# A graph layer with layer norm on one core: first adjacency block in two halves, scale factors of the last tiles in two chains

## The chip, the core and the metric

The kernel runs on one core of a Trainium2 chip. A core has TensorE (PE in the profile), VectorE (DVE), ScalarE (ACT), GpSimd (POOL) and SyncE (SP), each with its own stream of instructions; they wait for one another by semaphores. Sixteen DMA engines move data between HBM and the on-chip SBUF. TensorE writes to PSUM. The metric is the device time of one execution, in microseconds (us).

## What is computed

```python
support = x @ weight                      # x 4096x256, weight 256x256
y = (1 - t) * support + t * (adj @ support)   # adj 4096x4096, t one number
out = layernorm(x + y, axis=-1)           # eps 1e-5
```

## The kernel before

The product is reordered as z = t (adj x) + (1 - t) x, then z W. Each float32 operand is split into a high part of type fp32r (ScalarE or VectorE casts it) and a low part, the difference (VectorE, for early x GpSimd). A product is three matmuls: high by high, high by low, low by high. Output nodes are worked in 8 chunks of 512; per chunk the 32 blocks of 128 input nodes come in 8 groups of 4. One group is an adjacency tile of 1 MB in a ring of four slots (a_raw, a_hi, a_lo) and 24 matmuls of 512 columns into agg[chunk parity][feature half]. Chunks 0 and 1 alternate by group, so that x is used as it arrives.

At the start the first tiles come in small pieces. FIRST_RUN (L18) packs them in HBM in the order in which SyncE loads them (L204 to L221): x block 0, adjacency blocks 0 of slots 0 and 1, x block 1, and so on. Each has its own semaphore. Ten warm-up matmuls of 512 columns on constants (L675) stand ahead of the first useful one. The first adjacency block is loaded in one DMA; ScalarE casts its left 256 columns (L278), VectorE its right 256 (L469), VectorE subtracts all 512 (L464), and fine_piece (L565) issues six matmuls of 512 columns, with waits for hi, x_lo (GpSimd, L335) and lo between the pairs. The fifth piece (index 4) is the first that piece (L584) handles.

At the end project_last (L628) multiplies the last z by W in four tiles of 128 nodes; tiles 2 and 3 get the centred features added on TensorE by an identity matrix (L652, L653). VectorE adds the features of tiles 0 and 1 (L529), ScalarE sums their squares (L318), VectorE takes the statistics of tiles 2 and 3 (L533, L536). Then one chain works on a 128x4 array of all four tiles: VectorE adds eps (L539), takes the reciprocal (L541), multiplies by ScalarE's root (L544, L322) and does one Newton step (L546, L549). ScalarE scales tiles 2 and 3 (L325) and issues their stores (L329); VectorE scales 0 and 1 (L554) and SyncE issues theirs (L243).

The order on each engine is the order of the code; nothing reorders it.

Of the kernel before, what the change touches and what calls it, by code (L numbers as in the profile page):

```python
# [6 lines left out]
P = 128  # L7
WIDE = 512
GROUP = 4
# [3 lines left out]
WARM = 10  # L13
FINE = 4
# [9 lines left out]
def gnn_layernorm_kernel(nc, x_rows, first_run, xT, adjT, t, W, out):  # L24
# [33 lines left out]
    with ctx:  # L58
# [53 lines left out]
        first_hi_ready = sem("first_hi_ready")  # L112
# [26 lines left out]
        inv_var_ready = sem("inv_var_ready")  # L139
        act_stored = sem("act_stored")  # L140
# [19 lines left out]
        def adj_source(q):  # L160
            n = A_PIECES[q][2]
            first = run_offset("a", q)
            return first_run[first:first + n * P * WIDE].rearrange("(p b w) -> p b w", p=P, b=n)

        def load_and_store(sp):
# [12 lines left out]
            def load_adj(n):  # L178
                slot, turn = n % RING, n // RING
                c, g = chunk_group(n)  # L180
                if turn == 1:
                    sp.wait_ge(a0_lo_ready, a_after(slot))
# [22 lines left out]
            load_adj_piece(0)  # L205
# [40 lines left out]
            sp.wait_ge(stored[1], 16 * (CHUNKS // 2 - 1 + 2))  # L246
            sp.wait_ge(act_stored, 16 * 2)

        def scalar_engine(act):
# [22 lines left out]
            def root(c):  # L272
# [82 lines left out]
        def vector_engine(dve):  # L355
# [105 lines left out]

            def a_low_piece(q):
# [265 lines left out]
```

## Time and profile before

| what | us |
|---|---|
| median of 3 runs (lowest, highest) | 383.89 (383.85, 384.13) |
| the profiled execution's own time | 383.85 |
| its span in the trace | 382.6 |
| TensorE matmuls busy, 1686 instructions | 376.6 (98%) |
| VectorE busy | 237.6 (62%) |
| ScalarE busy | 145.7 (38%) |
| GpSimd busy | 22.2 (6%) |

Busy is the time in which an engine has an instruction running. Matmuls overlap: one of 512 columns is listed with 389 ns while the next begins after about 0.23 us, so the step between starts is what it costs. The transfers run at 258 to 420 GB/s over the first 57 us and at about half of that later. The granted TensorE clock is shown as full in all 40 slices; the pace of the first six microseconds is read from the steps between weight loads. PEld is the weight load, which overlaps the matmul before it; SPq and ACTq are the queues on which an engine issues DMAs.

### The profile page before, as it was taken

How to read it: one execution, taken by the hardware profiler on the slowest of the kernel's cores; microseconds unless marked ns; L12 is line 12 of the kernel's file. 1: busy time of each engine (PE TensorE's matmuls, PEld its weight loads, DVE VectorE, ACT ScalarE, POOL GpSimd, SP SyncE). 2: the span in 40 equal slices, each digit the busy share in tenths (PEclk: the TensorE clock that was granted, in tenths of full speed). 3: DMA queues.
4: the chain of work that ended last, by engine and by line, in shares of the span. 5: the costliest groups of instructions: out<-in, count | busy, mean ns of one | idle time of the engine just before them, and what ended most of it. 6: DMA issues, size and time to landing. Idle time of an engine off the chain costs nothing.

```text
span 382.6 us, 4167 instructions
## 1 busy us (share of the span) xinstructions
PE 376.6 (98%) x1686; PEld 310.8 (81%) x1686; DVE 237.6 (62%) x335; ACT 145.7 (38%) x114; POOL 22.2 (6%) x19
## 2 busy tenths in 40 slices
PE   9999999999999999999999999999999999999994
PEld 5888888888888888888888888888888888888884
DVE  4978955447879466844577446873477643697305
ACT  4767544243352434324424325244332344423102
POOL 1202300003000010000100001000100001000000
PEclk9999999999999999999999999999999999999999
DMA  7999997555465766557665666756647567321001
GB/s 258 418 392 418 415 420 265 190 217 207 179 231 208 257 217 233 184 214 258 218 202 194 208 244 212 243 197 213 212 179 274 174 267 270 119 106 55 2 0 56
DMA packets 19107, 84.42 MB, mean 221 GB/s; under 512 B 1936, under 2 KB 6800, under 8 KB 11408
## 3 DMA queue, kind: packets, MB, share of 16 engines
q1 hardware_dynamic: 18656, 83.89, 59.7%
q10 hardware_dynamic: 432, 0.26, 0.2%
q8 instruction: 13, 0.21, 0.2%
q14 instruction: 6, 0.05, 0.0%
HBM read 79.95 MB, written 4.19 MB: 220 GB/s over the span
## 4 chain that ended last, share of the span: by engine, by line
PE 98%; DVE 1%; ACT 0%; issue 0%; DVEq 0%
PE agg L563 30%; PE agg L562 30%; PE agg L561 30%; PE out_ps L624 3%; PE out_ps L625 2%; PE out_ps L676 1%; PE agg L573 1%; PE agg L577 1%; PE agg L581 0%; ACT x_raw L325 0%; DVE x_raw L529 0%; DVE stats L533 0%; PE out_ps L645 0%; PE out_ps L647 0%; PE out_ps L646 0%
## 5 line engine op out<-in xcount | busy, mean ns | idle before, releaser
L359 DVE TENSOR_TENSOR a_lo<-a_raw,a_hi 128x2048 fp32r<-128x2048 f32 x60 | 137.4, 2291 | 111.1 <-ACT a_hi L263 111.1
L561 PE MATMUL agg<-a_hi,x_hi 128*128 128x512 f32 x504 | 196.3, 389 | 0.0
L563 PE MATMUL agg<-a_hi,x_lo 128*128 128x512 f32 x504 | 196.2, 389 | 0.0
L562 PE MATMUL agg<-a_lo,x_hi 128*128 128x512 f32 x504 | 196.1, 389 | 0.0
L263 ACT ACTIVATE a_hi<-a_raw 128x2048 fp32r<-128x2048 f32 x60 | 114.7, 1913 | 129.0 <-PE agg L563 123.7
L561 PEld LDWEIGHTS agg<-a_hi,x_hi 128*128 128x128 f32 x504 | 94.6, 188 | 19.8
L563 PEld LDWEIGHTS agg<-a_hi,x_lo 128*128 128x128 f32 x504 | 94.6, 188 | 19.8
L562 PEld LDWEIGHTS agg<-a_lo,x_hi 128*128 128x128 f32 x504 | 94.6, 188 | 19.6
L340 POOL TENSOR_TENSOR xt<-xt,omt_col 128x1024 f32<-128x1024 f32 x8 | 18.1, 2257 | 292.4 <-DMA xt<-in_xT 292.4
L624 PE MATMUL out_ps<-w_split,z_hi 128*128 128x512 f32 x56 | 20.0, 397 | 0.0
L274 ACT ACTIVATE std<-var_eps 128x4 f32<-128x4 f32 x7 | 1.4, 206 | 47.7 <-DVE var_eps L400 47.7
L270 ACT ACTIVATE z_hi<-z 128x512 fp32r<-128x512 f32 x14 | 8.8, 633 | 26.8 <-DVE z L372 21.7
L625 PE MATMUL out_ps<-w_split,z_lo 128*128 128x256 f32 x56 | 15.7, 280 | 0.0
L464 DVE TENSOR_TENSOR a_lo<-a_raw,a_hi 128x512 fp32r<-128x512 f32 (+1 forms) x12 | 11.3, 961 | 2.6 <-ACT a_hi L257 2.2
L624 PEld LDWEIGHTS out_ps<-w_split,z_hi 128*128 128x128 f32 x56 | 10.5, 188 | 2.5
L372 DVE SCALAR_TENSOR_TENSOR z<-agg,t_col,xt 128x512 f32<-128x512 f32 x14 | 10.4, 747 | 2.8 <-PE agg L563 2.8
L378 DVE TENSOR_TENSOR z_lo<-z,z_hi 128x512 fp32r<-128x512 f32 x14 | 9.5, 688 | 2.7 <-ACT z_hi L270 2.1
L625 PEld LDWEIGHTS out_ps<-w_split,z_lo 128*128 128x128 f32 x56 | 10.6, 189 | 0.3
L428 DVE TENSOR_TENSOR x_lo<-x_raw,x_hi 128x1024 fp32r<-128x1024 f32 (+1 forms) x8 | 10.5, 1310 | 0.1
L257 ACT ACTIVATE a_hi<-a_raw 128x512 fp32r<-128x512 f32 (+1 forms) x11 | 8.7, 789 | 4.7 <-DMA a_raw<-in_first_run 4.6
L387 DVE TENSOR_TENSOR x_raw<-out_ps,rows 128x256 f32<-128x256 f32 x28 | 9.9, 416 | 0.0
L391 DVE TENSOR_TENSOR x_raw<-out_ps,x_raw 128x256 f32<-128x256 f32 x28 | 9.9, 415 | 0.0
(76 smaller groups left out, 95.9 us busy)
## 6 DMA issues: line engine op xcount, KB each, us to landing
a_raw<-in_adjT SPq DMA_DIRECT2D x60, 1024.0 KB, 4.8
xt<-in_xT SPq DMA_DIRECT2D x8, 512.0 KB, 5.6
rows<-in_x SPq DMA_DIRECT2D x8, 512.0 KB, 5.7
out<-x_raw SPq DMA_DIRECT2D x7, 512.0 KB, 2.9
x_raw<-in_first_run SPq DMA_DIRECT2D x6, 512.0 KB, 11.9
a_raw<-in_first_run SPq DMA_DIRECT2D x8, 256.0 KB, 4.6
a_raw<-in_first_run SPq DMA_DIRECT2D x4, 512.0 KB, 7.3
x_raw<-in_first_run SPq DMA_DIRECT2D x4, 128.0 KB, 3.9
```

The costliest lines, as they stand in the source:

```text
L263: nc.scalar.activation(a_hi[:, slot], a_raw[:, slot], ACT.Copy).then_inc(a_hi_ready[slot], 1)
L340: nc.gpsimd.tensor_tensor(xt[:, c % 2], xt[:, c % 2], omt_col[:, :].unsqueeze(2).broadcast_to([P, KT, WIDE]), ALU.mult).then_inc(xt_scaled, 1)
L359: nc.vector.tensor_tensor(a_lo[:, slot], a_raw[:, slot], a_hi[:, slot].bitcast(f32), ALU.subtract).then_inc(a_lo_ready[slot], 1)
L372: nc.vector.scalar_tensor_tensor(z[:, k], agg[c % 2][k][:, :], t_col[:, :], xt[:, c % 2, k], ALU.mult, ALU.add).then_inc(z_ready[k], 1)
L387: nc.vector.tensor_tensor(y_tile(i), out_ps[i][:, 0:feats], rows[:, c % 2, i], ALU.add).then_inc(part_ready, 1)
L428: nc.vector.tensor_tensor(x_lo[:, j:j + n], x_part(x_raw, p), x_hi[:, j:j + n].bitcast(f32), ALU.subtract).then_inc(x_lo_ready, 1)
L464: nc.vector.tensor_tensor(a_part(a_lo, q), a_part(a_raw, q), a_part(a_hi, q).bitcast(f32), ALU.subtract).then_inc(a0_lo_ready, 1)
L561: nc.tensor.matmul(bank, x_hi[:, j, cols], a_hi[:, slot, b], start=first, stop=False)
L562: nc.tensor.matmul(bank, x_hi[:, j, cols], a_lo[:, slot, b], start=False, stop=False)
L563: return nc.tensor.matmul(bank, x_lo[:, j, cols], a_hi[:, slot, b], start=False, stop=last)
L624: nc.tensor.matmul(out_ps[i][:, :], z_hi[:, k, cols], w_split[:, k], start=(k == 0), stop=False)
L625: done = nc.tensor.matmul(dst, z_lo[:, k, cols], w_hi[:, k], start=False, stop=(k == KT - 1))
```

## The change

The warm-ups become seven. The first adjacency block is stored in HBM as two blocks of 256 columns and loaded in two DMAs, each with a semaphore. VectorE casts half 0, ScalarE half 1, VectorE subtracts each, and TensorE does six matmuls of 256 columns on half 0 and then six on half 1. The counts of the waits on a0_hi_ready and a0_lo_ready move by one accordingly.

At the end the 128x4 chain becomes two 128x2 chains, for tiles 0 and 1 (early) and tiles 2 and 3 (late), with their rows alternating on VectorE, and two roots on ScalarE. ScalarE scales tiles 0 and 3, VectorE 2 and 1; SyncE stores 0, 2, 1 and ScalarE stores 3. One identity matmul of tile 3 moves behind the products of tile 2.

```diff
-WARM = 10
+WARM = 7
+HALF = WIDE // 2
...
             load_x(0)
-            load_adj_piece(0)
+            for h in range(2):
+                sp.dma_start(first_block(a_raw, h), first_block_source(h)).then_inc(half_loaded[h], 16)
             load_adj_piece(1)
...
-            for i in range(2):
-                sp.wait_ge(normed_ready, c * TILES + i + 1)
-                sp.dma_start(out[c * WIDE + i * P:c * WIDE + (i + 1) * P], normed(c)[:, i]
-                             ).then_inc(stored[c % 2], 16)
+            sp.wait_ge(act_normed_ready, 1)
+            sp.dma_start(out[c * WIDE:c * WIDE + P], normed(c)[:, 0]).then_inc(stored[c % 2], 16)
+            sp.wait_ge(normed_ready, c * TILES + 1)
+            sp.dma_start(out[c * WIDE + 2 * P:c * WIDE + 3 * P], normed(c)[:, 2]).then_inc(stored[c % 2], 16)
+            sp.wait_ge(normed_ready, c * TILES + 2)
+            sp.dma_start(out[c * WIDE + P:c * WIDE + 2 * P], normed(c)[:, 1]).then_inc(stored[c % 2], 16)
...
-            act.wait_ge(a0_loaded[0], 16)
-            nc.scalar.activation(a_hi[:, 0, 0, 0:WIDE // 2], a_raw[:, 0, 0, 0:WIDE // 2], ACT.Copy
-                                 ).then_inc(a0_hi_ready, 1)
+            act.wait_ge(half_loaded[1], 16)
+            nc.scalar.activation(first_block(a_hi, 1), first_block(a_raw, 1), ACT.Copy).then_inc(half_hi_ready[1], 1)
...
+            nc.scalar.activation(std[:, early], mean_var[:, early, 1], ACT.Sqrt, bias=eps_col[:, :]
+                                 ).then_inc(early_std_ready, 1)
             act.wait_ge(mean_var_ready, c * TILES + 2)
-            nc.scalar.activation(std[:, :], mean_var[:, :, 1], ACT.Sqrt, bias=eps_col[:, :]).then_inc(std_ready, 1)
+            nc.scalar.activation(std[:, late], mean_var[:, late, 1], ACT.Sqrt, bias=eps_col[:, :]).then_inc(std_ready, 1)
+            act.wait_ge(early_rstd_ready, 1)
+            nc.scalar.activation(normed(c)[:, 0], y_tile(0), ACT.Copy, scale=rstd[:, 0:1]).then_inc(act_normed_ready, 1)
             act.wait_ge(rstd_ready, c + 1)
-            for i in (2, 3):
-                nc.scalar.activation(normed(c)[:, i], out_ps[i][:, 0:feats], ACT.Copy, scale=rstd[:, i:i + 1]
-                                     ).then_inc(act_normed_ready, 1)
-            for i in (2, 3):
-                act.wait_ge(act_normed_ready, i - 1)
-                act.dma_start(out[c * WIDE + i * P:c * WIDE + (i + 1) * P], normed(c)[:, i]).then_inc(act_stored, 16)
+            nc.scalar.activation(normed(c)[:, 3], out_ps[3][:, 0:feats], ACT.Copy, scale=rstd[:, 3:4]
+                                 ).then_inc(act_normed_ready, 1)
+            act.wait_ge(act_normed_ready, 2)
+            act.dma_start(out[c * WIDE + 3 * P:c * WIDE + 4 * P], normed(c)[:, 3]).then_inc(act_stored, 16)
...
+            def a_low_half(h):
+                dve.wait_ge(half_hi_ready[h], 1)
+                nc.vector.tensor_tensor(first_block(a_lo, h), first_block(a_raw, h), first_block(a_hi, h).bitcast(f32),
+                                        ALU.subtract).then_inc(a0_lo_ready, 1)
+
...
             x_high(0)
-            dve.wait_ge(a0_loaded[0], 16)
-            nc.vector.tensor_copy(a_hi[:, 0, 0, WIDE // 2:], a_raw[:, 0, 0, WIDE // 2:]).then_inc(first_hi_ready, 1)
-            dve.wait_ge(first_hi_ready, 1)
-            a_low_piece(0)
+            dve.wait_ge(half_loaded[0], 16)
+            nc.vector.tensor_copy(first_block(a_hi, 0), first_block(a_raw, 0)).then_inc(half_hi_ready[0], 1)
+            for h in range(2):
+                a_low_half(h)
...
-            for i in (2, 3):
-                dve.wait_ge(stats_ready, c * TILES + i - 1)
-                nc.vector.bn_aggr(mean_var[:, i], stats[:, i]).then_inc(mean_var_ready, 1)
             dve.wait_ge(square_ready, 2)
+            nc.vector.tensor_scalar(var_eps[:, early], mean_var[:, early, 1], EPS, None, ALU.add
+                                    ).then_inc(early_var_ready, 1)
+            dve.wait_ge(stats_ready, c * TILES + 1)
+            nc.vector.bn_aggr(mean_var[:, 2], stats[:, 2]).then_inc(mean_var_ready, 1)
+            dve.wait_ge(early_var_ready, 1)
+            nc.vector.reciprocal(inv_var[:, early], var_eps[:, early]).then_inc(early_inv_ready, 1)
+            dve.wait_ge(stats_ready, c * TILES + 2)
+            nc.vector.bn_aggr(mean_var[:, 3], stats[:, 3]).then_inc(mean_var_ready, 1)
+            dve.wait_ge(early_inv_ready, 1)
+            dve.wait_ge(early_std_ready, 1)
+            nc.vector.tensor_tensor(rstd0[:, early], inv_var[:, early], std[:, early], ALU.mult
+                                    ).then_inc(early_rstd0_ready, 1)
             dve.wait_ge(mean_var_ready, c * TILES + 2)
-            nc.vector.tensor_scalar(var_eps[:, :], mean_var[:, :, 1], EPS, None, ALU.add).then_inc(var_eps_ready, 1)
+            nc.vector.tensor_scalar(var_eps[:, late], mean_var[:, late, 1], EPS, None, ALU.add).then_inc(var_eps_ready, 1)
+            dve.wait_ge(early_rstd0_ready, 1)
+            nc.vector.scalar_tensor_tensor(newton_q[:, early], std[:, early], -0.5, rstd0[:, early], ALU.mult, ALU.mult
+                                           ).then_inc(early_q_ready, 1)
             dve.wait_ge(var_eps_ready, c + 1)
-            nc.vector.reciprocal(inv_var[:, :], var_eps[:, :]).then_inc(inv_var_ready, 1)
+            nc.vector.reciprocal(inv_var[:, late], var_eps[:, late]).then_inc(inv_var_ready, 1)
+            dve.wait_ge(early_q_ready, 1)
+            nc.vector.scalar_tensor_tensor(rstd[:, early], newton_q[:, early], 1.5, rstd0[:, early], ALU.add, ALU.mult
+                                           ).then_inc(early_rstd_ready, 1)
             dve.wait_ge(inv_var_ready, 1)
             dve.wait_ge(std_ready, c + 1)
...
-            nc.vector.tensor_tensor(rstd0[:, :], inv_var[:, :], std[:, :], ALU.mult).then_inc(rstd0_ready, 1)
+            nc.vector.tensor_tensor(rstd0[:, late], inv_var[:, late], std[:, late], ALU.mult).then_inc(rstd0_ready, 1)
...
             dve.wait_ge(rstd_ready, c + 1)
             dve.wait_ge(stored[c % 2], 16 * (c // 2))
-            for i in (0, 1):
-                nc.vector.tensor_scalar(normed(c)[:, i], y_tile(i), rstd[:, i:i + 1], None, ALU.mult
-                                        ).then_inc(normed_ready, 1)
+            nc.vector.tensor_scalar(normed(c)[:, 2], out_ps[2][:, 0:feats], rstd[:, 2:3], None, ALU.mult
+                                    ).then_inc(normed_ready, 1)
+            dve.wait_ge(early_rstd_ready, 1)
+            nc.vector.tensor_scalar(normed(c)[:, 1], y_tile(1), rstd[:, 1:2], None, ALU.mult).then_inc(normed_ready, 1)
...
+            def first_piece_half(h):
+                cols = slice(h * HALF, (h + 1) * HALF)
+                pe.wait_ge(x0_hi_ready, 1)
+                pe.wait_ge(half_hi_ready[h], 1)
+                for k in range(KT):
+                    nc.tensor.matmul(agg[0][k][:, cols], x_hi[:, 0, k * P:(k + 1) * P], first_block(a_hi, h),
+                                     start=(h == 0), stop=False)
+                pe.wait_ge(x0_lo_ready, 1)
+                for k in range(KT):
+                    nc.tensor.matmul(agg[0][k][:, cols], x_lo[:, 0, k * P:(k + 1) * P], first_block(a_hi, h),
+                                     start=False, stop=False)
+                pe.wait_ge(a0_lo_ready, h + 1)
+                for k in range(KT):
+                    nc.tensor.matmul(agg[0][k][:, cols], x_hi[:, 0, k * P:(k + 1) * P], first_block(a_lo, h),
+                                     start=False, stop=False)
+
...
                 pe.wait_ge(x0_hi_ready, b + 1)
-                pe.wait_ge(a0_hi_ready, q + 1)
-                if q == 0:
-                    pe.wait_ge(first_hi_ready, 1)
+                pe.wait_ge(a0_hi_ready, q)
...
+                def add_features(i, part):
                     cols = slice((i - 2) * feats, (i - 1) * feats)
-                    nc.tensor.matmul(dst, ident[:, :], centred_part(a_hi)[:, cols], start=False, stop=False)
-                    nc.tensor.matmul(dst, ident[:, :], centred_part(a_lo)[:, cols], start=False, stop=False)
+                    nc.tensor.matmul(out_ps[i][:, 0:feats], ident[:, :], part[:, cols], start=False, stop=False)
...
-                for i in (2, 3):
-                    add_features(i)
+                add_features(2, centred_part(a_hi))
+                add_features(2, centred_part(a_lo))
+                add_features(3, centred_part(a_hi))
...
-                for i in (2, 3):
-                    high_times_weights(i)
-                    low_times_weights(i)
+                high_times_weights(2)
+                low_times_weights(2)
+                add_features(3, centred_part(a_lo))
+                high_times_weights(3)
+                low_times_weights(3)
...
             bf16 = mybir.dt.bfloat16
             for _ in range(WARM):
...
-            for q in range(FINE):
+            for h in range(2):
+                first_piece_half(h)
+            for q in range(1, FINE):
                 fine_piece(q)
```

On SyncE's queue at the start (128 partitions by elements per partition):

```order
L173 DMA x_raw<-in_first_run 128x256
L176 DMA a_raw<-in_first_run 128x512 x2
L173 DMA x_raw<-in_first_run 128x256
L176 DMA a_raw<-in_first_run 128x512 x2
L173 DMA x_raw<-in_first_run 128x256
```

and now

```order
L185 DMA x_raw<-in_first_run 128x256
L218 DMA a_raw<-in_first_run 128x256 x2
L188 DMA a_raw<-in_first_run 128x512
L185 DMA x_raw<-in_first_run 128x256
L188 DMA a_raw<-in_first_run 128x512 x2
L185 DMA x_raw<-in_first_run 128x256
```

Every load behind the first block stands one issue further back. On TensorE at the start, where agg00 and agg01 are the two feature halves of chunk 0, before

```order
L676 MATMUL out_ps0<-const-bfloat16-1.0 128x512 x10
L573 MATMUL agg00<-a_hi,x_hi 128x512
L573 MATMUL agg01<-a_hi,x_hi 128x512
L577 MATMUL agg00<-a_hi,x_lo 128x512
L577 MATMUL agg01<-a_hi,x_lo 128x512
L581 MATMUL agg00<-a_lo,x_hi 128x512
L581 MATMUL agg01<-a_lo,x_hi 128x512
```

and now

```order
L728 MATMUL out_ps0<-const-bfloat16-1.0 128x512 x7
L607 MATMUL agg00<-a_hi,x_hi 128x256
L607 MATMUL agg01<-a_hi,x_hi 128x256
L611 MATMUL agg00<-a_hi,x_lo 128x256
L611 MATMUL agg01<-a_hi,x_lo 128x256
L615 MATMUL agg00<-a_lo,x_hi 128x256
L615 MATMUL agg01<-a_lo,x_hi 128x256
L607 MATMUL agg00<-a_hi,x_hi 128x256
```

Six matmuls became twelve of half the width, the second six for half 1. On VectorE at the end, from the statistics of tile 3 on (out_ps3), before

```order
L533 BN_STATS stats<-out_ps3 128x6
L536 BN_AGGR mean_var<-stats 128x2 x2
L539 TENSOR_SCALAR var_eps<-mean_var 128x4
L541 RECIPROCAL inv_var<-var_eps 128x4
L544 TENSOR_TENSOR rstd0<-inv_var,std 128x4
L546 SCALAR_TENSOR_TENSOR newton_q<-std,rstd0 128x4
L549 SCALAR_TENSOR_TENSOR rstd<-newton_q,rstd0 128x4
L554 TENSOR_SCALAR x_raw<-x_raw,rstd 128x256 x2
```

and now

```order
L556 TENSOR_SCALAR var_eps<-mean_var 128x2
L559 BN_AGGR mean_var<-stats 128x2
L561 RECIPROCAL inv_var<-var_eps 128x2
L563 BN_AGGR mean_var<-stats 128x2
L566 TENSOR_TENSOR rstd0<-inv_var,std 128x2
L569 TENSOR_SCALAR var_eps<-mean_var 128x2
L571 SCALAR_TENSOR_TENSOR newton_q<-std,rstd0 128x2
L574 RECIPROCAL inv_var<-var_eps 128x2
L576 SCALAR_TENSOR_TENSOR rstd<-newton_q,rstd0 128x2
L580 TENSOR_TENSOR rstd0<-inv_var,std 128x2
L582 SCALAR_TENSOR_TENSOR newton_q<-std,rstd0 128x2
L585 SCALAR_TENSOR_TENSOR rstd<-newton_q,rstd0 128x2
```

Ten short rows stand where five stood, and two of the early chain's are ahead of the aggregation of tile 3 (L563).

## Rows read from the trace of the kernel before

**Rows 1.** The page: chain that ended last, by engine; costliest groups, one of TensorE's.
```profile
PE 98%; DVE 1%; ACT 0%; issue 0%; DVEq 0%
...
L561 PE MATMUL agg<-a_hi,x_hi 128*128 128x512 f32 x504 | 196.3, 389 | 0.0
```
**Rows 2.** Timeline (start us, length us, engine, line), 0 to 12 us, TensorE.
```profile
0.84 4.42 PE L676 MATMUL out_ps<-const-bfloat16-1.0 128*128 128x512 bf16 x10 [0.84 <-PEq L722]
...
4.63 0.33 PEld L573 LDWEIGHTS agg<-a_hi,x_hi 128*128 128x128 f32 x1 [0.28 <-issue]
5.06 0.33 PEld L573 LDWEIGHTS agg<-a_hi,x_hi 128*128 128x128 f32 x1
...
6.34 0.21 PEld L581 LDWEIGHTS agg<-a_lo,x_hi 128*128 128x128 f32 x1
6.61 0.19 PEld L581 LDWEIGHTS agg<-a_lo,x_hi 128*128 128x128 f32 x1
...
10.92 0.19 PEld L561 LDWEIGHTS agg<-a_hi,x_hi 128*128 128x128 f32 x1
11.14 0.39 PE L561 MATMUL agg<-a_hi,x_hi 128*128 128x512 f32 x1
```
**Rows 3.** Timeline, 0 to 5 us, the other engines.
```profile
1.25 0.42 SPq L176 DMA_DIRECT2D a_raw<-in_first_run  x1
1.71 0.42 SPq L176 DMA_DIRECT2D a_raw<-in_first_run  x1
...
2.95 0.29 DVE L423 CAST x_hi<-x_raw 128x256 fp32r<-128x256 f32 x1 [2.95 <-DMA x_raw<-in_first_run]
3.33 0.73 POOL L335 TENSOR_TENSOR x_lo<-x_raw,x_hi 128x256 fp32r<-128x256 f32 x1 [2.82 <-DVE x_hi L423]
3.79 0.42 ACT L278 ACTIVATE a_hi<-a_raw 128x256 fp32r<-128x256 f32 x1 [1.70 <-DMA a_raw<-in_first_run]
3.80 0.40 DVE L469 CAST a_hi<-a_raw 128x256 fp32r<-128x256 f32 x1 [0.55 <-DMA a_raw<-in_first_run]
```
**Rows 4.** Timeline, 7.7 to 10.7 us, pieces three and five.
```profile
7.76 0.69 DVE L464 TENSOR_TENSOR a_lo<-a_raw,a_hi 128x512 fp32r<-128x512 f32 x1 [1.26 <-ACT a_hi L257]
...
8.73 0.63 ACT L257 ACTIVATE a_hi<-a_raw 128x512 fp32r<-128x512 f32 x1 [0.36 <-DMA a_raw<-in_first_run]
...
9.38 0.74 POOL L335 TENSOR_TENSOR x_lo<-x_raw,x_hi 128x256 fp32r<-128x256 f32 x1 [2.06 <-DVE x_hi L423]
...
9.40 1.27 DVE L464 TENSOR_TENSOR a_lo<-a_raw,a_hi 128x512 fp32r<-128x512 f32 x1
```
**Rows 5.** Stretches; last columns: granted TensorE clock, DMA share, GB/s.
```profile
8.00:9.00 1.00, 1.00 (x6) 0.84 (x5) 1.00 (x2) 0.64 (x2) 0.00 (x0) 1.00 1.00 353
```
**Rows 6.** Timeline, 377 to 381 us, all engines.
```profile
377.20 0.28 PE L638 MATMUL out_ps<-w_split,z_lo 128*128 128x256 f32 x1
...
377.51 0.43 DVE L533 BATCH_NORM_STATS2 stats<-out_ps 128x6 f32<-128x256 f32 x1
...
377.86 0.30 DVE L536 BATCH_NORM_AGGREGATE mean_var<-stats 128x2 f32<-128x6 f32 x2
...
378.27 0.17 DVE L539 TENSOR_SCALAR var_eps<-mean_var 128x4 f32<-128x4 f32 x1
...
379.28 0.84 ACT L325 ACTIVATE x_raw<-out_ps,rstd 128x256 f32<-128x256 f32 x2 [0.72 <-DVE rstd L549]
...
379.66 0.34 SPq L243 DMA_DIRECT2D out<-x_raw  x1
...
380.05 0.43 SPq L243 DMA_DIRECT2D out<-x_raw  x1
...
380.17 0.45 ACTq L329 DMA_DIRECT2D out<-x_raw  x1
```
**Rows 7.** Chain of waits in order of time (start us, us), one product of tile 0.
```profile
376.05 0.12 PE out_ps L633
```
**Rows 8.** DMA view of 379 to 383 us, in 40 slices of 0.1 us.
```profile
GB/s 0 0 82 0 0 0 0 0 0 0 0 0 0 0 0 256 358 338 338 307 358 338 348 318 369 358 318 348 348 338 185 21 0 0 0 0 0 0 0 0
```

More of the change, by code:

```diff
@@ L110, in gnn_layernorm_kernel @@
         out_ps = [ctx.enter_context(nc.psum_tensor(f"out_ps{i}", [P, WIDE], f32)) for i in range(TILES)]
-        first_hi_ready = sem("first_hi_ready")
+        half_loaded, half_hi_ready = sems("half_loaded", 2), sems("half_hi_ready", 2)
         w_loaded, w_hi_ready, w_lo_ready = sem("w_loaded"), sem("w_hi_ready"), sem("w_lo_ready")
@@ L139, in gnn_layernorm_kernel @@
         inv_var_ready = sem("inv_var_ready")
+        early_var_ready, early_inv_ready, early_std_ready = sem("early_var_ready"), sem("early_inv_ready"), sem("early_std_ready")
+        early_rstd0_ready, early_q_ready, early_rstd_ready = sem("early_rstd0_ready"), sem("early_q_ready"), sem("early_rstd_ready")
         act_stored = sem("act_stored")
@@ L149, in x_part, with first_block @@
             return buf[:, j // GROUP % X_RING, j % GROUP:j % GROUP + n]
+        def first_block(buf, h):
+            return buf[:, 0, 0, h * HALF:(h + 1) * HALF]
         def run_offset(kind, index):
@@ L163, in adj_source, with first_block_source @@
             return first_run[first:first + n * P * WIDE].rearrange("(p b w) -> p b w", p=P, b=n)
+        def first_block_source(h):
+            first = run_offset("a", 0) + h * P * HALF
+            return first_run[first:first + P * HALF].rearrange("(p w) -> p w", p=P)
+        early, late = slice(0, 2), slice(2, TILES)
         def load_and_store(sp):
@@ L181, in load_adj @@
                 if turn == 1:
-                    sp.wait_ge(a0_lo_ready, a_after(slot))
+                    sp.wait_ge(a0_lo_ready, a_after(slot) + 1)
                 else:
@@ L543, in vector_engine @@
             dve.wait_ge(std_ready, c + 1)
-            nc.vector.tensor_tensor(rstd0[:, :], inv_var[:, :], std[:, :], ALU.mult).then_inc(rstd0_ready, 1)
+            nc.vector.tensor_tensor(rstd0[:, late], inv_var[:, late], std[:, late], ALU.mult).then_inc(rstd0_ready, 1)
             dve.wait_ge(rstd0_ready, c + 1)
-            nc.vector.scalar_tensor_tensor(newton_q[:, :], std[:, :], -0.5, rstd0[:, :], ALU.mult, ALU.mult
+            nc.vector.scalar_tensor_tensor(newton_q[:, late], std[:, late], -0.5, rstd0[:, late], ALU.mult, ALU.mult
@@ L547, in vector_engine @@
                                            ).then_inc(newton_q_ready, 1)
             dve.wait_ge(newton_q_ready, c + 1)
-            nc.vector.scalar_tensor_tensor(rstd[:, :], newton_q[:, :], 1.5, rstd0[:, :], ALU.add, ALU.mult
+            nc.vector.scalar_tensor_tensor(rstd[:, late], newton_q[:, late], 1.5, rstd0[:, late], ALU.add, ALU.mult
                                            ).then_inc(rstd_ready, 1)
@@ L578, in fine_piece @@
                                      start=False, stop=False)
-                pe.wait_ge(a0_lo_ready, q + 1)
+                pe.wait_ge(a0_lo_ready, q + 2)
                 for k in range(KT):
@@ L586, in piece @@
                 c, g = chunk_group(slot)
-                pe.wait_ge(a0_lo_ready, q + 1)
+                pe.wait_ge(a0_lo_ready, q + 2)
                 if g == 0:
@@ L716 @@
             slot, b, n = A_PIECES[index]
-            first_run.append(adjT[slot % 2 * (blocks // GROUP) + slot // 2, :, b:b + n].ravel())
+            halves = [slice(0, HALF), slice(HALF, WIDE)] if index == 0 else [slice(0, WIDE)]
+            for cols in halves:
+                first_run.append(adjT[slot % 2 * (blocks // GROUP) + slot // 2, :, b:b + n, cols].ravel())
     first_run = np.concatenate(first_run)
```

8 lines of the change are left out of this document (3 added, 5 removed).

## The prediction, made before the changed kernel ran

> **What bounds the kernel now.** I read the page's chain of waits first. TensorE holds 98% of it, and in the costliest groups its matmuls show no idle time before them [rows 1]. So a microsecond counts only where TensorE works slowly or has nothing to do: ahead of the steady stream, and after its last matmul. The timeline of the first 12 us shows the first. Ten warm-up matmuls on constants start at 0.84 us; weight loads then follow at the pace of one 512-column matmul, 0.43 us (4.63 to 5.06), and still do to 6.34; from 6.34 to 6.61 the step is 0.27 us, and afterwards it is 0.23 (10.92 to 11.14 is one step) [rows 2]. 512 columns in 0.43 us is the 1.2 GHz level, in 0.22 us the 2.4 GHz level; the rise lies near 6.4 us, after 5.5 us of unbroken matmuls. Useful work begins in the array at 5.06 us.
>
> The timeline of the end shows the other: the last matmul ends at 377.20 + 0.28 = 377.48 us, and the span at 382.6. Those 5.1 us are the normalisation of the last four tiles on VectorE and ScalarE, and the stores [rows 6]. So at most about 6 us are open to this change; the rest is 5.44 us per 24 matmuls, which it leaves alone.
>
> **Warm-ups and halves.** Three warm-ups fewer free 3 x 0.43 = 1.28 us of slow time: the seven end at 5.06 - 1.28 = 3.78 us. At half pace that is worth 0.64 us at most, and only if data are there at once. They are not. In the kernel before, x is seen at 2.95 and the 256 KB block at 3.80 [rows 3]. Half 0 is 128 KB behind x; half of that 0.85 us gives 3.38 us. Its cast runs on VectorE. The same cast of x took 0.29 us, the one of the block 0.40, beside GpSimd's x_lo, which runs from 3.33 to 4.06 [rows 3]. The same pair shows again at 9.4: a subtraction of 512 columns takes 0.69 us alone and 1.27 us when x_lo started 0.02 us before it, ending 0.55 us after x_lo's end [rows 4]. That is not slowing in proportion; VectorE stood still until GpSimd was done. So the half's cast, started at 3.38 against x_lo at 3.33, should end about 0.15 us after 4.06, at 4.2, where it ended before. If it wins by arriving earlier, it ends at 3.7. I take 4.2. The Trainium skill (SBUF — State Buffer, "Who interferes with whom") states this as a lock: whichever of the two starts first holds the shared port pair for its whole instruction, and the other fully blocks. The trace agrees, in both places; by a proportional sharing of the port the cast would end at about 3.9 and TensorE would begin 0.3 us earlier.
>
> TensorE then gets half 0 at 4.24, streams from about 4.45 (a weight load of 0.33 us lies ahead of the first matmul), and has idled some 0.6 us. Against 5.06 this is 0.6 us earlier at half pace: 0.3 us in full-speed terms. Twelve matmuls of 256 columns carry the columns of six of 512. At the fast level one of 256 steps by 0.12 us [rows 7] against 0.23 for 512, so each split costs 0.01: at most 6 x 0.01 = 0.06, and I take 0.03. The other inputs are in time: x_lo at 4.06, half 1 by ScalarE at 3.79 + 0.42 = 4.21 or one more landing later, a_lo of half 0 some 0.45 us after 4.2, needed at 4.9. Head start at the second block: 0.27 us (0.1 to 0.6).
>
> **What the head start meets.** Pieces keep arriving at the pace of the transfers. The tightest one is the fifth adjacency piece. ScalarE idles 0.36 us for its landing and splits it at 8.73; VectorE's a_lo of it starts at 9.40, behind x_lo as told above, and is ready at 10.67; TensorE's weight load for it goes at 10.92 and its matmul streams at 11.14 [rows 2, 4]. Weight loads run one matmul ahead; with an idle array about 0.1 us of it is enough. So TensorE could have started that piece at 10.67 + 0.05 + 0.1 = 10.82 in place of 11.14: 0.3 us is the most that a head start can bring through here, if the piece comes no later. It comes later: the halves are one more DMA and rows of 1 KB instead of 2 KB. From below this costs 0: four stores of 128 KB in 1 KB rows moved in 1.7 us, 0.42 each [rows 8], and two of them equal the block's 0.85. From above it costs the spacing of two issues on SyncE's queue, 0.46 us (1.25 to 1.71) [rows 3]. The transfer engines are full in these microseconds (share 1.00 in 8 to 9 us) [rows 5], so the issue hides in their backlog and I take 0.15 for row overhead and one more completion. The piece is then ready at 10.97 and its matmul streams near 11.0 to 11.05: the gain that passes is 0.1 us (-0.15 to +0.3). Behind this place the pieces are needed every 1.36 us and come faster; nothing else is near. The steady stream then runs unchanged, 0.1 us earlier.
>
> **The tail.** TensorE's last work: one matmul on the identity moves from ahead of tile 0's products to ahead of tile 3's. Tiles 0 to 2 end 0.12 us earlier [rows 7], tile 3 not at all. VectorE's statistics of tile 3 start at 377.51, 0.03 us after TensorE's end at 377.48 [rows 6], so they stay. From there VectorE had two aggregations from 377.86, five dependent steps of 0.20 us each from 378.27, and the scaling at 379.28. Now the first aggregation has a row of tiles 0 and 1 ahead of it, and a reciprocal that itself waits 0.2 us stands ahead of the second, which so starts near 378.13 in place of 377.98. The five late steps follow with the early chain's rows in the 0.2 us gaps: late factors 0.1 us later (0 if all hides, 0.3 if each of five inserted rows adds 0.06), so scaling at 379.38. Early factors are ready near 378.88, 0.4 us before the old ones.
>
> Stores before: issues at 379.66 and 380.05 on SyncE, the last at 380.17 on ScalarE [rows 6]. Data move from 380.5 to 382.2 without a pause [rows 8]: 0.85 us after the first issue, 0.42 us per tile. The rate of the transfers, not the last issue, sets the end. Now: ScalarE scales tile 0 from 378.88, SyncE issues it at 379.33; tile 2 follows at 379.38 + 0.38 = 379.76 (the lag of scaling to issue in rows 6), tile 3 from ScalarE at 379.38 + 0.52 = 379.90 (one scaling of about 0.47, two take 0.84, and 0.05 to the issue), tile 1 at 379.76 + 0.46 = 380.22. Data: tile 0 from 380.18 to 380.60, where tile 2 is just ready, then three times 0.42: 381.87. Tile 1 could have begun at 381.07 and doesn't decide. Gain 382.2 - 381.87, less a little for holes between issues: 0.27 us (0 to 0.4).
>
> **Sum.** 383.85 (this execution, span 382.6 and 1.25 around it) - 0.1 - 0.27 = 383.48; the median of the runs, 383.89, gives 383.52. Forecast 383.5, own range 383.2 to 383.8.
>
> **Rivals.** (a) Both ends pay in full: the fifth piece arrives no later or its subtraction misses x_lo (0.58 us less), the head start is 0.45, the tail 0.35: 383.85 - 0.8 = 383.05. For it: the block's time equals two halves of a store. Against it: the order of VectorE's rows around that piece is the same. (b) The tail gives nothing: three stores in one queue, the last issued at 380.22 or, with the longer chain, 380.4, against 380.17. If the end tracks the last issue, it is 0.05 to 0.2 us later: 383.85 - 0.1 + 0.1 = 383.85. For it: the last store landed 2.0 us after its issue. Against it: the unbroken transfer of rows 8. (c) Slower: the clock. TensorE now idles some 0.6 us between warm-ups and half 0. Before, the rise came after 5.5 us of unbroken matmuls. If the hole makes it come 5.5 us after 4.1, at 9.6 in place of 6.4, TensorE works 5.15 us at half pace (4.45 to 9.6), 2.6 us of full-speed work; before it had done 0.67 + 3.2 = 3.9 by then. It is 1.3 us behind, less the tail's 0.27: 384.85. It decides from a rise about 0.8 us late on. For it: no warm-up matmul covers the hole. Against it: the hole is a tenth of those microseconds. The Trainium skill (TensorE: Matmul & The Clock Gate, "What you observe") has the rise around 4 us into sustained matmuls, give or take 0.5 us from run to run; this trace shows 5.5 us. A rise 0.5 us late would cost 0.25 us at the second block, most of which the wait for the fifth piece absorbs.
>
> **How the numbers follow.** This kernel's runs tell a change from none at about 0.2%, 0.77 us: faster is below 383.12, slower above 384.66. Forecast 54%, (a) 17%, (b) 20%, (c) 9%. Forecast and (b) are no change; (a) is spread around the bound, and I give 16% to faster in all; (c) all slower: 0.16, 0.75, 0.09. The range takes in (a), (b) and small delays of the clock: 382.9 to 384.05.
>
> **What would show it.** Right: the half's cast ends near 4.2 us; TensorE idles after the seventh warm-up; its step halves near 6.4; a wait appears ahead of the fifth piece near 10.9; from 12 us on TensorE is 0.1 us earlier; the second aggregation starts 0.6 us after tile 3's statistics; data of the stores end 4.4 us after TensorE's last matmul, against 4.7. Wrong: a cast at 3.7 us with no hole; no wait at the fifth piece and a gain of 0.4 us or more by 12 us; steps of 0.43 us beyond 7 us; a pause in the transfers of the stores.

## The result and the profile after

The changed kernel is slower: 384.04 us median (383.48 to 384.79, 22 runs) against 383.62 us (382.88 to 384.13, 22 runs of before), ratio 1.0015, 95% interval 1.0009 to 1.0021. (The 383.89 shown earlier was the median of three of these.) The forecast was 383.5, that is 0.37 us less than the 383.89 it started from, with 0.75 on no change and 0.09 on slower; 384.04 lies at the upper edge of its range (384.05). Measured side by side the change costs 0.42 us by the medians and 0.6 us by the ratio, which is clear of noise and still less than the 0.2% from which the prediction counts a change as slower. A few executions of these series took far longer at a granted clock well below full, one of two_dma_2k for instance 639.53 us and the profiled one of tail_act_35 878.59; the ratios leave them out. The changed kernel's profiled execution took 384.10 us, span 382.9, against 383.85 and 382.6.

The chain of waits (shares by engine, then by line) no longer belongs to TensorE alone:

```profile
PE 96%; DMA 1%; DVE 1%; SPq 1%; issue 0%; ACT 0%
```

Before it read PE 98% [rows 1]. The new links are in the first 12 us. The chain of the stretches 2 to 7 and 9 to 12.5 us, in order of time (start us, us, what):

```profile
1.71 0.42 SPq L218
...
4.07 0.43 SPq L185
...
4.55 4.85 DMA a_raw<-in_first_run
...
9.42 0.64 ACT a_hi L272
...
10.09 1.24 DVE a_lo L485
...
11.37 0.50 PE agg L598
```

It starts at the issue of half 1, runs through SyncE's issues to the load of the fifth piece, and from there through its two splits to TensorE. The timeline (start us, us, engine, line; in brackets idle time before and what ended it) has the rows that answer to [rows 2 to 4]:

```profile
3.29 0.72 POOL L351 TENSOR_TENSOR x_lo<-x_raw,x_hi 128x256 fp32r<-128x256 f32 x1 [2.79 <-DVE x_hi L439]
3.44 0.73 DVE L490 CAST a_hi<-a_raw 128x256 fp32r<-128x256 f32 x1 [0.22 <-DMA a_raw<-in_first_run]
...
4.31 0.55 PE L607 MATMUL agg<-a_hi,x_hi 128*128 128x256 f32 x1 [0.33 <-DVE a_hi L490]
...
6.37 0.33 PEld L615 LDWEIGHTS agg<-a_lo,x_hi 128*128 128x128 f32 x1
6.59 0.26 PEld L615 LDWEIGHTS agg<-a_lo,x_hi 128*128 128x128 f32 x1
6.78 0.19 PEld L624 LDWEIGHTS agg<-a_hi,x_hi 128*128 128x128 f32 x1
...
9.42 0.63 ACT L272 ACTIVATE a_hi<-a_raw 128x512 fp32r<-128x512 f32 x1 [0.40 <-DMA a_raw<-in_first_run]
...
10.09 1.23 DVE L485 TENSOR_TENSOR a_lo<-a_raw,a_hi 128x512 fp32r<-128x512 f32 x1
...
11.37 0.50 PE L598 MATMUL agg<-a_hi,x_hi 128*128 128x512 f32 x1 [0.23 <-DVE a_lo L485]
```

The cast of half 0 took 0.73 us beside GpSimd and ended at 4.17. The first useful matmul is listed from 4.31, and the second weight load, which marks the first matmul in the array, goes at 4.45; before it went at 5.06 [rows 2]. So useful work began 0.6 us earlier, at the 1.2 GHz level. The step of a 256-column matmul is 0.21 to 0.22 us until 6.59, 0.19 there and shorter after. The first matmul of the second block shows what is left of the head start. Changed kernel, then the kernel before:

```profile
6.89 0.40 PE L624 MATMUL agg<-a_hi,x_hi 128*128 128x512 f32 x1
...
7.07 0.39 PE L573 MATMUL agg<-a_hi,x_hi 128*128 128x512 f32 x1
```

That is 0.18 us. (The weight loads for these two, at 6.78 and 6.84, can't be compared: each goes one matmul ahead, and the matmul between has 256 columns in one kernel and 512 in the other.) The fifth piece was split from 9.42, before from 8.73: 0.69 us later. TensorE waited and reached it at 11.37 in place of 11.14. Its weight load came with that matmul in place of ahead of it, and the end of the last matmul is 377.90, before 377.48: 0.42 us later.

The end of the kernel, rows that answer to [rows 6]:

```profile
377.62 0.28 PE L689 MATMUL out_ps<-w_split,z_lo 128*128 128x256 f32 x1
...
377.93 0.43 DVE L554 BATCH_NORM_STATS2 stats<-out_ps 128x6 f32<-128x256 f32 x1
...
378.55 0.16 DVE L563 BATCH_NORM_AGGREGATE mean_var<-stats 128x2 f32<-128x6 f32 x1
...
379.73 0.48 DVE L589 TENSOR_SCALAR x_raw<-out_ps,rstd 128x256 f32<-128x256 f32 x1
...
379.79 0.34 SPq L255 DMA_DIRECT2D out<-x_raw  x1
...
380.24 0.36 SPq L257 DMA_DIRECT2D out<-x_raw  x1
...
380.65 0.45 SPq L259 DMA_DIRECT2D out<-x_raw  x1
```

and the DMA view of 379 to 383 us in slices of 0.1 us [rows 8]:

```profile
GB/s 0 0 0 0 0 0 0 0 0 0 0 0 0 0 0 0 174 317 358 317 123 215 358 348 328 348 338 338 328 328 348 358 267 51 0 0 0 0 0 0
```

Data move from 380.6 to 382.4, with a dent at 381.0 where tile 0 has gone and tile 2 has not yet come. They end 4.5 us after TensorE's last matmul, before 4.7. Start and end together: +0.42 - 0.15 = +0.27 of the span.

### The profile page after: what moved, and what is told of

Same layout as the page of the kernel before. It is cut to its first block, busy times and chain, and to the rows that moved or that the text cites. A ratio compares the mean times of both kernels' runs of the same rounds, so it can differ in the third digit from the quotient of the medians.

```text
span 382.9 us, 4180 instructions
## 1 busy us (share of the span) xinstructions
PE 376.5 (98%) x1689; PEld 311.1 (81%) x1689; DVE 239.0 (62%) x341; ACT 146.2 (38%) x115; POOL 22.5 (6%) x19
## 4 chain that ended last, share of the span: by engine, by line
PE 96%; DMA 1%; DVE 1%; SPq 1%; issue 0%; ACT 0%
PE agg L598 30%; PE agg L600 30%; PE agg L599 30%; PE out_ps L675 3%; PE out_ps L676 2%; DMA a_raw<-in_first_run 1%; SPq L188 0%; SPq L185 0%; DVE a_lo L485 0%; SPq L218 0%; ACT a_hi L272 0%; PE out_ps L684 0%; PE out_ps L689 0%; DVE x_raw L589 0%; PE out_ps L696 0%
## 5 line engine op out<-in xcount | busy, mean ns | idle before, releaser
L433 DVE TENSOR_SCALAR x_raw<-x_raw,mean_var,rstd 128x256 f32<-128x256 f32 x28 | 9.7, 409 | 0.3
```

## Experiments

"Issued" is the time at which SyncE issues the load of the fifth piece, "fifth" the start of ScalarE's split of it, "rise" the time at which the step of TensorE halves, "GB/s" what the transfers moved from 2 to 7 us, "last" the end of the last matmul, each in the one profile of the kernel. Ratios are to the kernel before on the same chip. One profile is one execution: that of one_dma_1k, for instance, is the slowest of its eleven runs (384.16 us, median 383.66).

| kernel | ratio (95%) | rise | issued | fifth | GB/s | last |
|---|---|---|---|---|---|---|
| before | 1 | 6.4 | 4.07 | 8.73 | 303 | 377.48 |
| the change | 1.0015 (1.0009-1.0021) | 6.7 | 4.55 | 9.42 | 273 | 377.90 |
| tail_only | 0.9992 (0.9984-1.0001) | 5.4 | 4.06 | 8.41 | 310 | 377.03 |
| tail_again | 1.0002 (0.9993-1.0011) | 5.8 | 4.07 | 8.16 | 313 | 377.26 |
| start_only | 1.0016 (1.0007-1.0025) | 4.8 | 4.55 | 9.22 | 237 | 377.65 |
| start_warm10 | 1.0015 (1.0007-1.0024) | 6.7 | 4.54 | 10.54 | 251 | 378.47 |
| warm7_only | 1.0003 (0.9990-1.0016) | 8.7 | 4.06 | 8.96 | 308 | 378.40 |
| warm4_only | 1.0043 (1.0028-1.0058) | 8.5 | 4.07 | 8.70 | 307 | 378.31 |
| one_dma_1k | 1.0002 (0.9994-1.0011) | 6.0 | 4.10 | 9.45 | 303 | 377.82 |
| one_load | 1.0003 (0.9994-1.0012) | 3.7 | 4.07 | 8.56 | 318 | 377.00 |
| two_dma_2k | 1.0024 (1.0015-1.0033) | 6.7 | 4.98 | 9.59 | 210 | 378.03 |
| extra_small | 1.0015 (1.0006-1.0024) | 5.9 | 4.35 | 9.56 | 260 | 377.97 |
| start_xlo | 1.0019 (1.0010-1.0027) | 4.1 | 4.54 | 9.01 | 260 | 377.48 |
| two_dma_act | 1.0015 (1.0006-1.0023) | 4.0 | 4.58 | 9.99 | 204 | 378.47 |
| half1_act | 1.0038 (1.0026-1.0051) | 9.0 | 4.05 | 8.87 | 271 | 378.54 |
| after_act | 1.0020 (1.0006-1.0034) | 8.8 | 3.59 | 9.10 | 310 | 378.93 |
| after_act10 | 0.9999 (0.9990-1.0008) | 5.3 | 3.59 | 8.37 | 325 | 377.15 |
| tail_act | 0.9997 (0.9988-1.0006) | 3.7 | 3.64 | 8.61 | 305 | 376.99 |
| after_merge | 1.0029 (1.0017-1.0040) | 4.6 | 4.11 | 9.42 | 224 | 378.33 |
| tail_act_35 | 1.0026 (1.0014-1.0039) | - | - | - | - | - |

**Which half costs.** tail_only and tail_again are the kernel before with only the lines of the diff on the last four tiles (roots, chains, scalings, stores, identity matmul); start_only has all its other lines and the old end.

> Only the last four tiles are changed (two chains, stores, identity matmul); the start is that of before. Theory S (the start costs, the tail gives): 0.2 us less than before, ratio near 0.9995; the data of the last stores end about 4.5 us after TensorE's last matmul against 4.7. Theory T (the tail costs, for instance by its third store in one queue): 0.3 to 0.5 us more. In its profile the first piece of TensorE's wait at the fifth adjacency piece is absent, as before.

> The changed end with the start of before, once more. If the end gives 0.2 to 0.3 us: ratio 0.9992 to 0.9995 again, and below 1 with the first measurement together. If the first was chance: 1.0000.

> Only the start is changed (two half loads, seven warm-ups, twelve matmuls of 256 columns); the end is that of before. Theory S: 0.6 us more than before (0.42 for the whole change and the 0.2 that the tail gives back), with the fifth piece's landing 0.5 to 0.7 us later than 8.7 us and TensorE waiting for it. Theory T: within 0.1 us of before. Theory R (the late landings in the profile are chance of one run): landings spread over the same times as before, time within 0.1 us.

The start costs all of it: ratio 1.0016, 384.00 us against 383.63, which is 0.4 us by the medians and 0.6 by the ratio. Its profile has the same late fifth piece (9.22), but there TensorE loses more at the third: its weight load for that one goes at 8.25 after 1.19 us of idling, and the wait at the fifth is 0.32 us. The end is between -0.3 us and nothing: the two ratios average 0.9997. From TensorE's last matmul to the end of the span pass 4.95 to 4.96 us in the seven profiles with the new end, 5.08 to 5.15 in ten with the old one (5.34 in two more); that is a gain of 0.15 us, less than the first run suggested.

**Warm-ups or loads.** start_warm10 and warm7_only:

```diff
-WARM = 7        # start_only -> start_warm10
+WARM = 10
-WARM = 10       # before -> warm7_only
+WARM = 7
```

> The changed start with ten warm-ups, the end of before. If the loads are what costs, TensorE again waits at the fifth piece and the time is that of start_only within 0.1 us (about 0.6 us above before). If the missing three warm-ups are what costs (clock), the time is near before.

> The kernel before with seven warm-ups in place of ten. If the clock's rise depends on unbroken work, it comes later than 6.4 us and the time is 0.3 us or more above before. If not, TensorE idles from 3.8 to 4.25 us, starts useful work 0.3 us earlier in full-speed terms than with ten, and the wait at the fifth piece takes all but about 0.3 us of it: 0.0 to 0.3 us less than before.

With ten warm-ups the changed start is as slow as with seven (384.16 and 384.00). With the old loads, seven cost nothing on average (383.63), but the runs spread from 382.79 to 385.76, and the profile, of an execution of 384.75 us, has the rise at 8.7 us. So the loads cost, and the warm-ups leave something else behind, taken up below.

**Rows, halves or one more DMA.** one_dma_1k keeps one DMA and makes its rows 1 KB; two_dma_2k keeps the rows and makes two DMAs; one_load has the halved work on one load; extra_small adds a DMA that carries next to nothing.

```diff
-            load_adj_piece(0)                                   # one_dma_1k
+            sp.dma_start(a_raw[:, 0, 0].rearrange("p (h w) -> p h w", h=2), ...rearrange("(h p w) -> p h w", h=2, p=P))
-            load_adj_piece(0)                                   # two_dma_2k
+            for h in range(2):
+                sp.dma_start(a_part(a_raw, 0)[part], adj_source(0)[part]).then_inc(a0_loaded[0], 16)
-            for h in range(2):                                  # start_only -> one_load
-                sp.dma_start(first_block(a_raw, h), first_block_source(h)).then_inc(half_loaded[h], 16)
+            load_adj_piece(0)
             load_adj_piece(0)                                   # extra_small
+            sp.dma_start(spare[0:1, :], first_run[0:P].rearrange("(p w) -> p w", p=1)).then_inc(spare_loaded, 16)
```

> The kernel before, with the first block laid out in HBM as two half blocks and loaded by one DMA, so 256 rows of 1 KB in place of 128 of 2 KB, with no further issue. Theory Rows (the 1 KB rows cost the time between 3 and 4 us): 0.4 to 0.6 us more than before, and about 150 KB moved in that microsecond in place of 290 to 370. Theory Issue (the second DMA of the block costs it): within 0.1 us of before.

> The kernel before, with the first block loaded in two DMAs of 64 partitions each, rows of 2 KB kept, so every later load is issued 0.46 us later. Theory Issue: 0.4 to 0.6 us more than before and the trough between 3 and 4 us. Theory Rows: within 0.1 us of before.

> The changed start with seven warm-ups and the halves in casts and matmuls, but the block loaded whole in one DMA with rows of 2 KB; the end of before. Both theories of the load: the time of before within 0.15 us, no wait of TensorE at the fifth piece beyond 0.1 us. If the halved work itself costs (twelve matmuls, casts apart): 0.3 us or more above before.

> The kernel before with one more DMA on SyncE behind the first block that moves 512 bytes in one row to a spare place. Theory Count: 0.5 to 0.9 us more, as with the block in two DMAs (ratio 1.0024). Theory Split: within 0.1 us of before.

The 1 KB rows cost nothing (1.0002), nor do the halved casts and matmuls (1.0003). One expectation of one_load did not come: with its early rise (3.7) TensorE was early enough to wait at the fifth piece, its weight load idling 0.61 us. The second DMA costs it all, with 2 KB rows too (1.0024); there SyncE's issues drew apart as well (1.19 us for the two halves), so that its later loads came 0.9 us later and not the 0.46 expected. Even a DMA of 512 bytes costs 0.54 us (383.99 against 383.45). Timeline of extra_small:

```profile
1.70 0.33 SPq L208 DMA_DIRECT2D spare<-in_first_run  x1
...
8.62 0.19 PEld L577 LDWEIGHTS agg<-a_hi,x_hi 128*128 128x128 f32 x1 [0.64 <-issue]
...
9.56 0.64 ACT L261 ACTIVATE a_hi<-a_raw 128x512 fp32r<-128x512 f32 x1 [0.40 <-DMA a_raw<-in_first_run]
...
11.51 0.19 PEld L565 LDWEIGHTS agg<-a_hi,x_hi 128*128 128x128 f32 x1 [0.28 <-DVE a_lo L468]
```

The issue took a slot of 0.37 us and SyncE issued the fifth piece 0.28 us later, yet that piece came 0.83 us later than before. TensorE waited twice: first and longer at the third piece, which ScalarE could split only from 7.87 (before 7.10), then at the fifth.

**Whose slot.** two_dma_act and half1_act are meant to leave the later loads of SyncE where they were, with the second part issued by ScalarE; after_act and tail_act move the second piece there as well, so that SyncE issues one load fewer. after_merge takes one DMA away. tail_act_35 moves two later pieces to ScalarE.

```diff
+            act.dma_start(a_part(a_raw, 0)[P // 2:P], ...)      # two_dma_act; half1_act: first_block(a_raw, 1)
+            act.dma_start(a_part(a_raw, 1), adj_source(1))...   # after_act (behind half 1), tail_act
-            load_adj_piece(2)                                   # after_merge
-            load_adj_piece(3)
+            sp.dma_start(a_raw[:, 0:2, 1], ...rearrange("(s p w) -> p s w", s=2, p=P)).then_inc(a0_loaded[2], 16)
+            act.dma_start(a_part(a_raw, 3), ...)                # tail_act_35, and 5
```

> The kernel before, first block in two DMAs of 64 partitions, the second one issued by ScalarE at 0.8 us, so SyncE's later loads keep their places. Theory Queue (what costs is the 0.46 us by which SyncE issues everything later): within 0.1 us of before. Theory Count (one more DMA in the rings costs, whoever issues it): 0.5 to 0.9 us more, as with both on SyncE (384.40).

> The changed start with the end of before, half 1 issued by ScalarE at 0.8 us. Theory Queue: 0.5 us less than the changed start alone (384.0), so about 383.5, and the fifth piece lands near 8.7 us. Theory Count: 384.0.

> The whole change, with half 1 and the second piece issued by ScalarE, so SyncE issues one load fewer than in the kernel before. Theory Queue: the later loads are issued 0.46 us earlier than before, TensorE's wait at the fifth piece goes, and with the tail's 0.3 us the time is 0.4 to 0.7 us below before: 382.9 to 383.2. Theory Count: 384.0 as the whole change.

> The changed end with the start of before, the second piece issued by ScalarE at 0.8 us. Theory Queue: the fifth piece lands 0.3 to 0.5 us earlier than 8.4 to 8.7 us; TensorE did not wait there with ten warm-ups, so the time is that of the changed end alone, 383.2 within 0.15 us, and its chance delays get rarer. Theory Count: the same time, the same landing.

> The whole change, with the third and fourth adjacency pieces loaded in one DMA, so the number of DMAs ahead of the fifth piece is that of the kernel before. Theory Count: the fifth piece is ready 0.5 us earlier than with the whole change (11.3 us), the time is 0.3 to 0.5 us below 384.04, near 383.6. Theory Split (what costs is that the first block arrives in two parts, whatever follows): 384.0.

> The changed end, ten warm-ups, the whole first block; pieces 3 and 5 are issued by ScalarE behind its table load, at 2.1 and 2.5 us, so SyncE's later loads come 0.46 and 0.93 us earlier. If issue slots set the landings: the fifth piece (index 4) lands at 8.3 us or earlier against 8.4 to 8.9, waits of TensorE get rarer, the time is 0.1 to 0.3 us below the changed end alone. If the bytes in flight set them: the same landing, the same time as the changed end alone.

two_dma_act did not do what it was meant to. SyncE's issues from the half block on drew apart to steps of 0.60 to 0.68 us, as in two_dma_2k:

```profile
1.25 0.55 SPq L205 DMA_DIRECT2D a_raw<-in_first_run  x1
1.85 0.58 SPq L176 DMA_DIRECT2D a_raw<-in_first_run  x1
2.47 0.65 SPq L173 DMA_DIRECT2D x_raw<-in_first_run  x1
```

so the fifth piece was issued at 4.58, as late as in the changed kernel (4.55), and 1.0015 with a fifth piece at 9.99 says nothing against Theory Queue. half1_act did keep SyncE's issues in place (4.05), and its fifth piece came at 8.87, near the 8.7 of Theory Queue; its time (385.06 us, 1.0038) is not the forecast 383.5, and its rise is at 9.0 us, of which more below. after_act missed its forecast as well (384.75), again with a late rise (8.8). after_act10 has one DMA more than the kernel before, but SyncE issues one load fewer: 0.9999, fifth piece at 8.37. So the count of DMAs alone is not the answer.

The issue time parts the ten kernels that have ten warm-ups and a row in the table: fifth piece issued at 4.10 or earlier, ratio 0.9992 to 1.0002 (the kernel before, tail_only, tail_again, one_dma_1k, after_act10, tail_act) and 303 to 325 GB/s; issued at 4.35 or later, 1.0015 to 1.0024 (start_warm10, two_dma_2k, extra_small, two_dma_act) and 204 to 260 GB/s. This leans to Theory Queue, but the loss is larger than the slot: extra_small issues 0.28 us later and lands 0.83 us later. Nor does an earlier issue give anything: tail_act issued the fifth piece at 3.64, it came at 8.61, and the time is that of the changed end alone. after_merge has the number of DMAs and the issue time (4.11) of the kernel before and still kept 9.42, but it had a new wait of its own, TensorE standing 1.8 us at the third piece, which now landed with the fourth. tail_act_35 did not set up its case: ScalarE issued the two pieces at 0.83 and 1.24 us, its table load did not hold them back, and they went ahead of and along with the first block, issued by SyncE at 1.23; of its profile only such issues of the first microseconds are read, and its ratio of 1.0026 stands outside the parting above. That a DMA more on SyncE ahead of the early pieces costs is shown; why it costs more than its slot is open.

**The pause of the clock.** warm4_only is the kernel before with WARM = 4; after_act10 is after_act with WARM = 10.

> The kernel before with four warm-ups: TensorE idles from 2.5 to 4.25 us. If the hole delays the rise, most runs have it at 7 us or later and lie above 384.3; ratio 1.002 or more. If only the onset of work counts, the time is within 0.1 us of before, as with seven warm-ups (383.63), and no run lies above 384.3.

> As the kernel with half 1 and the second piece on ScalarE's queue (384.75, and three of twelve runs at 383.0 to 383.3), but ten warm-ups, so TensorE works without a pause. Theory Clock: the slow group goes, median 383.1 to 383.5, rise below 7 us in the profile. Theory Loads: median stays at 384.5 or more, and TensorE waits in the profile at a piece.

Both came as the clock theory said. Timeline of warm4_only, weight loads:

```profile
4.49 0.29 PEld L573 LDWEIGHTS agg<-a_hi,x_hi 128*128 128x128 f32 x1 [2.69 <-issue]
...
7.65 0.33 PEld L577 LDWEIGHTS agg<-a_hi,x_lo 128*128 128x128 f32 x1
8.07 0.33 PEld L577 LDWEIGHTS agg<-a_hi,x_lo 128*128 128x128 f32 x1
8.50 0.21 PEld L581 LDWEIGHTS agg<-a_lo,x_hi 128*128 128x128 f32 x1
8.76 0.19 PEld L581 LDWEIGHTS agg<-a_lo,x_hi 128*128 128x128 f32 x1
```

Steps of 0.43 us until 8.5, 2 us longer than before, and all its runs at 384.6 or more. after_act had three runs of twelve at 383.0 to 383.3 and eight at 384.5 or more; with ten warm-ups the eleven runs lie between 382.8 and 383.8. Over all profiles, the rise came at 3.7 to 6.7 us in ten with ten warm-ups, and at 8.7 to 9.0 in three of eight with seven.

**The standstill of VectorE.** start_xlo computes the early low parts of x on VectorE.

```diff
+            def x_low_early(p):
+                nc.vector.tensor_tensor(x_lo[:, j:j + n], x_part(x_raw, p), x_hi[:, j:j + n].bitcast(f32), ALU.subtract)
```

> The changed start, end of before, with the low parts of x blocks 0 to 3 computed by VectorE in place of GpSimd. If VectorE stands still while GpSimd reads, the cast of half 0 takes 0.29 us in place of 0.73 to 0.83, the subtraction of the fifth piece 0.69 in place of 1.24, and TensorE's wait there is 0.2 us shorter: 0.2 us less than the changed start alone (384.0), still above before. If the two share in proportion, the sum of VectorE's work grows by 4 x 0.43 us and nothing is gained.

The rows came as expected, the time not:

```profile
3.32 0.30 DVE L488 CAST a_hi<-a_raw 128x256 fp32r<-128x256 f32 x1 [0.19 <-DMA a_raw<-in_first_run]
...
6.46 0.19 PEld L608 LDWEIGHTS agg<-a_hi,x_hi 128*128 128x128 f32 x1 [1.06 <-issue]
...
8.74 0.19 PEld L612 LDWEIGHTS agg<-a_hi,x_lo 128*128 128x128 f32 x1 [0.59 <-DVE x_lo L436]
...
9.68 0.69 DVE L483 TENSOR_TENSOR a_lo<-a_raw,a_hi 128x512 fp32r<-128x512 f32 x1 [0.19 <-ACT a_hi L268]
```

0.30 in place of 0.73, 0.69 in place of 1.23. In start_only, where the cast came first (3.35, x_lo 3.39), it took 0.29 and the next subtraction 0.83 in place of 0.42, GpSimd's x_lo 0.84 in place of 0.73. But 384.36 us is not below 384.0: in its profile (383.82 us, the fastest of its runs) TensorE waits 1.06 us at the second piece, which ScalarE could split only from 5.72 (5.41 in the changed kernel), and 0.59 us at the third, for an x_lo that now stands in VectorE's queue; and its last matmul ends at 377.48, where it ended before the change.

## Why the prediction was wrong

**The step that failed** is this one: "The transfer engines are full in these microseconds ..., so the issue hides in their backlog and I take 0.15". It was written with 0.46 us as its upper bound. Measured: 0.69 us between the two profiles, and a start that costs 0.4 to 0.6 us in time. The issue did not hide. SyncE's issues of the fifth and sixth pieces, the kernel before and the changed one:

```profile
4.07 0.91 SPq L176 DMA_DIRECT2D a_raw<-in_first_run  x2
...
4.55 0.91 SPq L188 DMA_DIRECT2D a_raw<-in_first_run  x2
```

The issue came 0.48 us later and all of it was passed on; from issue to split took 0.21 us more on top (4.87 in place of 4.66). It is not one profile's chance: with SyncE's queue of before and rows of 2 KB the fifth piece was split at 8.16 to 8.96 in six profiles, with the changed start's queue at 9.01 to 10.54 in four. (one_dma_1k with 9.45 stands outside, in its slowest run.) The premise was wrong too: a busy share near 1.00 doesn't say how much data flow. The stretch from 3 to 4 us, columns as in [rows 5], of the kernel before:

```profile
3.00:4.00 1.00, 1.00 (x4) 0.37 (x3) 0.45 (x2) 0.20 (x1) 0.67 (x1) 1.00 1.02 289
```

and of the changed kernel:

```profile
3.00:4.00 1.00, 0.98 (x3) 0.08 (x1) 0.78 (x2) 0.00 (x0) 0.71 (x1) 1.00 0.96 136
```

The share is 1.02 at 289 GB/s and 0.96 at 136. The rows of 1 KB and the halved work, the other parts of that term, cost nothing (one_dma_1k, one_load). The fifth piece was named rightly as the place that decides, and so was the wait there; its lateness had the wrong size, and with it the sign of the whole. That "nothing else is near" holds for the changed kernel's profile, but not for its neighbours: in start_only, extra_small and two_dma_act TensorE waited longest at the third piece. By the prediction's own arithmetic the fifth piece 0.69 late gives 10.67 + 0.15 + 0.69 = 11.51 against 11.14 (0.15 are its terms from subtraction to matmul), a loss of 0.37 us; measured 0.42 at the last matmul.

**Head start.** 0.27 us forecast at the second block, 0.18 found; TensorE's first useful matmul was in the array at 4.45, as forecast, but the rise came at 6.7 in place of 6.4. It did not matter here: TensorE then waited for the fifth piece, and start_warm10 is as slow without the head start.

**VectorE against GpSimd.** Right: forecast 4.2 us for the end of the cast, found 4.17. The Trainium skill (SBUF — State Buffer, "Who interferes with whom") has this as an exclusive lock, and start_only's opposite order, in which the cast ran free and the others waited, agrees: 0.83 us for the subtraction and 0.84 us for x_lo.

**Tail.** Direction right, size half: 0.27 forecast, 0.15 found. The late factors came when forecast or sooner (scaling 1.80 us after tile 3's statistics, before 1.77). The term that was too small is the scaling of tile 2: I took 0.38 from scaling to issue, the lag of a tile in SBUF; from PSUM the scaling alone takes 0.48, the issue came 0.51 us after its start, and the transfers ran dry for 0.1 us.

**Rival (c), the clock,** had 9%. As a mechanism it is shown, by warm4_only and after_act10, in the direction described; it is not what slows the changed kernel in most runs, since the time is the same with ten warm-ups. Seven warm-ups without the extra load would come out even, with a wide spread. **Rival (a)** needed the fifth piece on time and is refuted for this kernel. **Rival (b)**, a tail that gives nothing, is refuted by the trace, though not by the times.

No version tried beats the kernel before clear of noise. The changed end with the old start is the best by the trace; its two ratios straddle 1.

## What to carry to other kernels

At the start of a kernel, count the DMAs that one queue issues ahead of the pieces that the bottleneck engine waits for; one more small one cost 0.5 us here, while halving rows from 2 KB to 1 KB cost nothing. A head start is worth only what the tightest later piece lets through: find it by the slack of each piece, and of the next tightest, before pricing the head start. Read in the trace whether an experiment moved what it was meant to move, and only that: two_dma_act did not. Fewer warm-ups are safe only if useful matmuls follow without a pause; average times hide it, the spread shows it.

## What the runs showed of the hardware

- The rise of TensorE's clock is not at a fixed time even in the same kernel start: 3.7 to 6.7 us in ten profiles with ten warm-ups. The Trainium skill (TensorE: Matmul & The Clock Gate, "What you observe") gives 0.5 us of spread either way; these profiles show 1.5 us either way.
- A pause of TensorE before the rise can put it off. Counted from the last warm-up's end (3.78 us with seven, 2.5 with four) to the first useful weight load, pauses of 0.76 us (warm7_only), 0.82 (half1_act), 1.64 (after_act) and 2.0 (warm4_only) went with rises at 8.5 to 9.0 us; the shorter ones of the changed kernel (0.50) and after_merge (0.44) did not.
- 512 bytes in one more early DMA on SyncE: +0.54 us, ratio 1.0015 (1.0006 to 1.0024).
- A DMA share of 0.96 at 136 GB/s and of 1.02 at 289 GB/s, both from 3 to 4 us: the share is no measure of throughput.
- Each load of SyncE takes a slot of 0.47 us from issue to issue; where the first block was split by partitions, the slots of its halves and of the next loads were 0.60 to 0.68 (two_dma_act, two_dma_2k). Why is open.
- ScalarE's DMA issues are not held back by its table load (tail_act_35: an issue at 0.83 us beside a table load from 0.80 to 2.08).
